# Two Fourier layers in one kernel: the projection of layer 1 takes sum and difference of its two terms

## What is computed

```python
a = x_ft[:, :, :nm, :nm]                      # 32 x 32 modes of the image
blk1 = _complex_matmul_2d(a, fw1)             # [B, O, 32, 32]
blk2 = _complex_matmul_2d(a, fw2)
out_ft = out_ft.at[:, :, :nm, :nm].set(blk1)
out_ft = out_ft.at[:, :, N - nm:, :nm].set(blk2)
out = jnp.fft.irfft2(out_ft, s=(N, M)) / scale_bwd
res = out @ W + b
return jax.nn.relu(res + out)
```

## Time and profile before

| | us |
|---|---|
| median of 3 runs (lowest, highest) | 2138.09 (2133.49, 2140.34) |
| time of the profiled execution | 2134.44 |
| its span in the profile | 2132.6 |
| the part from load 2's issue (763) to the last load's first mix (1018) | 255 |
| from there to the end of the last projections (1046) | 28 |

### The profile page before, as it was taken

How to read it: one execution, slowest core, us unless ns; L and a number is a source line. 1 busy time by engine, 2 the same in 40 slices (tenths; PEclk the granted TensorE clock), 3 DMA queues, 4 the chain that set the end, 5 groups by cost and what they waited for, 6 DMA issues and landing times.

```text
span 2132.6 us, 57900 instructions
## 1 busy us (share of the span) xinstructions
PE 1878.7 (88%) x24558; PEld 1494.5 (70%) x24558; DVE 1426.5 (67%) x2151; ACT 1144.2 (54%) x1869; POOL 282.8 (13%) x526
## 2 busy tenths in 40 slices
PE   5898998999639678888559999999999999999999
PEld 3676766777524567777447888878878788887887
DVE  5876776677144742222267888878888788887887
ACT  5755665556114311111146776666767666776665
POOL 0000000000000210000131304032040501404000
PEclk9999999999855579989879999999999999999999
DMA  8887887786296589999338888888788888888886
GB/s 305 312 262 237 277 266 227 251 271 204 62 155 80 117 238 265 257 264 273 90 127 289 293 301 325 305 321 297 277 310 307 321 307 282 299 305 307 315 308 244
DMA packets 210172, 546.88 MB, mean 256 GB/s; under 512 B 64322, under 2 KB 139586, under 8 KB 173634
## 3 DMA queue, kind: packets, MB, share of 16 engines
q1 hardware_dynamic: 150866, 458.18, 64.0%
q10 hardware_dynamic: 53680, 41.95, 8.0%
q0 software_dynamic: 5376, 43.07, 6.9%
HBM read 361.68 MB, written 148.96 MB: 239 GB/s over the span
## 4 chain that ended last, share of the span: by engine, by line
PE 41%; DMA 8%; DVE 1%; POOL 0%; issue 0%; DVEq 0%; POOLq 0%
PE ps_y L1406 13%; PE ps_xt L1353 9%; PE ps_wave L1392 9%; DMA x_in<-in_x 7%; PE ps_col L1373 5%; PE ps_y L1396 4%; DVE by_channel L770 1%; DVE low_tile L1296 0%; DMA tile<-high_tile 0%; DMA planes_in<-planes 0%; POOL tile L1223 0%; POOL planes_in L1211 0%; DVE by_channel L771 0%; DVE y_out L1325 0%; POOL low_tile L1223 0%
## 5 line engine op out<-in xcount | busy, mean ns | idle before, releaser
L1255 ACT ACTIVATE x_turned<-ps_xt 128x512 f16<-128x512 f32 x512 | 305.6, 597 | 320.4 <-PE ps_xt L1353 320.4
L1406 PE MATMUL ps_y<-apply,x_turned 128*128 128x128 f16 x6144 | 427.9, 219 | 0.0
L1406 PEld LDWEIGHTS ps_y<-apply,x_turned 128*128 128x128 f16 x6144 | 377.2, 98 | 64.5 <-issue 0.5
L1304 DVE TENSOR_TENSOR x_turned<-ps_xt,x_turned 128x512 f16<-128x512 f32 x512 | 351.6, 687 | 94.4 <-ACT x_turned L1255 94.4
L221 DVE TENSOR_TENSOR parts<-stage,parts 128x1024 f16<-128x1024 f32 x256 | 302.0, 1220 | 121.4 <-ACT parts L145 120.9
L1325 DVE SCALAR_TENSOR_TENSOR y_out<-ps_y,relu 128x512 f32<-128x512 f32 x512 | 351.5, 687 | 21.5 <-PE ps_y L1406 1.9
L1353 PE MATMUL ps_xt<-c_eye,x_in 128*128 128x128 f32 x2048 | 311.4, 275 | 10.6 <-DMA x_in<-in_x 10.6
L1265 ACT ACTIVATE relu<-ps_wave 128x512 f32<-128x512 f32 x512 | 303.4, 593 | 14.4 <-PE ps_wave L1392 14.4
L145 ACT ACTIVATE parts<-stage 128x1024 f16<-128x1024 f32 x256 | 255.1, 1049 | 78.8 <-issue 42.5
L290 PE MATMUL row_ps<-parts,c_rows_dft 128*64 128x512 f16 x1536 | 201.8, 391 | 62.8 <-DVE parts L221 53.1
L1296 DVE SCALAR_TENSOR_TENSOR low_tile<-ps_col,high_tile 128x512 f16<-128x512 f32 x248 | 171.1, 691 | 92.2 <-ACT high_tile L1248 92.2
(11 more groups left out here) (129 smaller groups left out, 1888.4 us busy)
## 6 DMA issues: line engine op xcount, KB each, us to landing
stage<-in_x SPq DMA_DIRECT2D x256, 512.0 KB, 4.9
x_in<-in_x SPq DMA_DIRECT2D x128, 1024.0 KB, 10.9
out_y<-y_out SPq DMA_DIRECT2D x128, 1024.0 KB, 7.0
fw_first<-in_fw SPq DMA_DIRECT2D x9, 2048.0 KB, 16.3
fw<-in_fw ACTq DMA_DIRECT2D x8, 2048.0 KB, 19.4
fw<-in_fw SPq DMA_DIRECT2D x8, 2048.0 KB, 17.5
fw_first<-in_fw ACTq DMA_DIRECT2D x7, 2048.0 KB, 20.4
tile<-high_tile POOLq DMA_DIRECT2D x48, 240.0 KB, 13.6
```

Source lines behind the costliest of these rows:

```text
L1255: nc.scalar.activation(turned[u % 2][:, 0, :, :], ps_turn[u % 2][:, :, :], ACT.Copy).then_inc(turn_high, 1)
L1304: nc.vector.tensor_tensor(v[:, 1, :, :], ps_turn[u % 2][:, :, :], v[:, 0, :, :], ALU.subtract).then_inc(turn_split, 1)
L1406: mm = nc.tensor.matmul(ps_y[u % 2][:, :, 2 * k:2 * k + 2], turned[u % 2][:, p, k, :], apply[:, bass.ds(b, 1), q, :, :].rearrange("p o c w ...
```

## The change

The first term and the second term of a frequency k go into the cosine row as their sum and into the sine row as their difference. Before, one matmul for each term made both rows, with 256 columns in `table`. Now DVE makes the sum and the difference (`add`, two instructions on 128x512 f32, into two new buffers `mix_sums`), and a matmul makes one row (h = 0 from the sum, h = 1 from the difference) with 128 columns. The number of matmuls per frequency stays 8; frequency 0 has no second term and reads `mix_turned` as before, frequency 32 has no first term and gets a copy and a negated copy. `table` is half as large. Then the order within a step changes on each engine:

```diff
+            def add(k):
+                if k == 0:
+                    return
+                n = sums_number(k)
+                for f in terms(k):
+                    dve.wait_ge(turn_taken, 2 * (slot_of(f, k) + 1))
+                if n >= 2:
+                    dve.wait_ge(out_ready, number[[j for j in order if j != 0][n - 2]] + 1)
...
+                    nc.vector.tensor_tensor(to[:, 0, :], first, second, ALU.add)
+                    nc.vector.tensor_tensor(to[:, 1, :], first, second, ALU.subtract).then_inc(sums_ready, 1)
@@ sync
             for step in range(STEPS + 8):
+                if step % KC == KC - 1 and step // KC + SL < LOADS:
+                    load(sp, 0, step // KC + SL)
                 for blk in flush_at(step):
                     store(sp, blk, 0, stored)
-                if step % KC == KC - 1 and step // KC + SL < LOADS:
-                    load(sp, 0, step // KC + SL)
@@ scalar
             for step in range(STEPS + 8):
-                for k in project_at(step):
-                    take_high(k)
-                for blk in flush_at(step):
-                    store(act, blk, 1, stored_sin)
                 slot = turn_at(step)
                 if slot is not None:
                     take_turn(slot)
                 if step % KC == KC - 1 and step // KC + SL < LOADS:
                     load(act, 1, step // KC + SL)
+                for k in project_at(step):
+                    take_high(k)
+                for blk in flush_at(step):
+                    store(act, blk, 1, stored_sin)
@@ vector
             for step in range(STEPS + 8):
+                if step < STEPS:
+                    take_mixed(step)
                 for k in project_at(step):
                     take_low(k)
-                if step < STEPS:
-                    take_mixed(step)
+                for k in project_at(step + 1):
+                    add(k)
@@ tensor, project(k)
+                if k == 0:
+                    pe.wait_ge(turn_taken, 2 * (slot_of(0, 0) + 1))
+                else:
+                    pe.wait_ge(sums_ready, sums_number(k) + 1)
...
                 for bh in range(2):
...
+                    for h in range(2):
+                        for r in range(2):
+                            v = turned(slot_of(0, 0))[:, 0] if k == 0 else sums[sums_number(k) % 2][:, h]
+                            last = nc.tensor.matmul(
+                                ps_out[n % 2][:, bh, :, h, :], v[:, r, bh * HB:(bh + 1) * HB, :].rearrange("p b y -> p (b y)"),
+                                table[:, r, h, :, :], start=(r == 0),
+                                stop=(r == 1 and (k, h) != (0, 0)))
@@ tensor
             for step in range(STEPS + 8):
-                for k in project_at(step):
-                    project(k)
                 slot = turn_at(step)
                 if slot is not None:
                     turn(slot)
                 if step < STEPS:
                     mix(step)
+                for k in project_at(step):
+                    project(k)
```

More of the change, by code:

```diff
@@ L837, in mix_project @@
         out = [m.sb(f"project_out{i}", [P, 2, 2, 2, 2, FLUSH, C], F16) for i in range(2)]
-        table = m.sb("project_table", [P, 2, 2, 2, 2, C])
+        sums = [m.sb(f"mix_sums{i}", [P, 2, 2, B, K1]) for i in range(2)]
+        table = m.sb("project_table", [P, 2, 2, 2, C])
         W_eye = m.sb("W_eye", [P, C])
@@ L861, in mix_project, with sums_number @@
         block = m.stack.enter_context(nc.Block())
+        def sums_number(k):
+            return number[k] - (number[0] < number[k])
         def turned(slot):
@@ L932, in take_turn @@
                         before = slot - KC if slot % KC else slot - 2 * KC
+                        if before == 0:
+                            act.wait_ge(out_ready, number[0] + 1)
                         if before >= 0:
-                            act.wait_ge(out_ready, max(number[k] for k in range(K1 + 1) for f in terms(k)
-                                                       if slot_of(f, k) == before) + 1)
+                            act.wait_ge(sums_ready, max(sums_number(k) for k in range(1, K1 + 1) for f in terms(k)
+                                                        if slot_of(f, k) == before) + 1)
                     y0 = i * MG // 2
@@ L1000, in _ @@
                 nc.vector.tensor_tensor(W_eye[half, :], w["W"][half, :], w["eye"][half, half], ALU.add).then_inc(table_cleared, 1)
-            nc.vector.memset(table[:, :, :, :, :, :], 0.0).then_inc(table_cleared, 1)
+            nc.vector.memset(table[:, :, :, :, :], 0.0).then_inc(table_cleared, 1)
             nc.vector.memset(first_y[:, :], 0.0).then_inc(table_cleared, 1)
             dve.wait_ge(table_cleared, 4)
[L1004 to L1011, removed]
+            for r in range(2):
+                for part in range(2):
+                    for h in range(2):
+                        half, g = slice(part * C, (part + 1) * C), (r + part + h) % 2
+                        minus = (r, part) == (1, 1) if h == 0 else (r, part) == (0, 0)
+                        nc.vector.tensor_scalar(table[half, r, h, g, :], W_eye[half, :], -1.0 if minus else 1.0, None,
+                                                ALU.mult).then_inc(table_ready, 1)
             nc.vector.memset(first_y[:, 0::K1], 1.0).then_inc(table_ready, 1)
@@ L1063, in project @@
                 for bh in range(2):
[L1064 to L1069, removed]
-                            stop=((f, r) == pairs[-1] and k > 0))
-                    if k == 0:
-                        last = nc.tensor.matmul(ps_out[n % 2][:, bh, 0, 0, :], first_y[0:1, :], bias_n[0:1, :],
-                                                start=False, stop=True)
+                    for h in range(2):
+                        for r in range(2):
+                            v = turned(slot_of(0, 0))[:, 0] if k == 0 else sums[sums_number(k) % 2][:, h]
[3 more added lines that the diff above has]
+                                stop=(r == 1 and (k, h) != (0, 0)))
+                        if (k, h) == (0, 0):
+                            last = nc.tensor.matmul(ps_out[n % 2][:, bh, 0, 0, :], first_y[0:1, :], bias_n[0:1, :],
+                                                    start=False, stop=True)
                 last.then_inc(out_ready, 1)
             for step in range(STEPS + 8):
-                for k in project_at(step):
-                    project(k)
                 slot = turn_at(step)
```

12 lines of the change are left out of this document (9 added, 3 removed).

## The result

| | before | after |
|---|---|---|
| median of 6 runs each, us (lowest, highest) | 2136.45 (2132.76, 2144.38) | 2154.95 (2149.24, 2166.13) |
| ratio after to before, 95% interval | | 1.0086 (1.0054 to 1.0117) |
| the profiled execution, us; its span | 2134.44; 2132.6 | 2154.77; 2152.8 |
| load 1's issue to the issue of the last stores, from SP's queue | 298.2 | 321.5 |

The changed kernel is slower, as forecast: the forecast was +12.9 us, the medians say +18.5. Inside the block the traces differ by 23.3 us; the stages before it were 3.4 us shorter in that execution (load 1's issue at 743.86 instead of 747.30), so all of the loss is in the block.

What follows compares the result with a forecast made beforehand. Bound: the loop of group, release and transfer through two weight buffers, paced by even groups. Terms 11.9 - 5.0 + 3.2 + 5.6 - 2.0 - 0.8 = +12.9 us gave 2147.3 (median 2151), range 2128 to 2172.

Steps and rivals of the forecast that it cites:

- Projection, pair, chain: PE's projection takes 1.94 us, DVE's pair 1.30, the serial chain from one projection's hand-over to the next's start 2.77.
- Even group: On PE, an even load's group now holds three projections and two chains: 13.8 us against 12.1, +11.9 over seven.
- Clock and stalls: Four more even groups start at 1.2 GHz on PE, +5.6 us; some unexplained stalls fall into idle time, -2.0.
- The two even groups that did not wait for weights: PE arrives 4.6 us earlier per chunk, worth 2.5 at each of these two groups: -5.0.
- Stores ahead of the load: Stores issue about 0.25 us behind the release instead of 0.8 ahead; the load behind is 1.05 later, three times: +3.2.
- End: From the last load's first mix to the issue of the last stores: 26.4 us instead of 27.2, -0.8.
- PE's own work sets the pace: Rival: PE's path over a chunk falls from 30.1 to 27.2 us, so faster, 2120 to 2127; chance 0.23.
- Swallowed: Rival: stalls lie in the new gaps, clock stays up, stores cost nothing; no change, 2138 to 2144; chance 0.18.
- The clock falls inside the groups: Rival: one more projection in each even group runs at 1.2 GHz, 13.6 us on top, 2165; chance 0.17.

Runs made afterwards that it cites:

- e5: The changed kernel with PE's waits ahead of even groups 6, 8, 10, 12 and 14 filled with matmuls that nobody reads; 2151.64 us, 1.0081 of before.
- e1: The changed kernel with DVE making the next frequency's sum and difference ahead of this one's eviction; 2135.81 us, 0.9989 of before.
- e2: The changed kernel with two more DVE instructions ahead of each pair, written to a buffer nobody reads; 2182.48 us, 1.0197 of before.
- e3: The kernel before with only the new order within a step, no sums; 2167.82 us, 1.013 of before.
- e4: The changed kernel (sums and differences) with the old order within a step; 2131.07 us, 0.9968 of before.
- e8: e4 with the pair for the next frequency ahead of this one's eviction on DVE; 2127.35 us, 0.9962 of before.
- e10: e8 with all stores of the 64 steps on SP's queue, a step later, behind the load; 2125.98 us, 0.993 of before.
- e11: The changed kernel with all stores of the 64 steps on SP's queue, behind the load; 2140.66 us, 1.0004 of before.
- e9: e4 with the stores issued one step later on both SP's and ACT's queues, behind the load; 2152.67 us, 1.0081 of before.
- e12: The kernel before, without sums, with all stores of the 64 steps on SP's queue, behind the load; 2136.65 us, 0.9997 of before.
- e6: The changed kernel with the stores issued one step later on both SP's and ACT's queues, behind the load; 2151.33 us, 1.0065 of before.

## Why the prediction was right in sign and 5.6 us short

**Projection, pair, chain: right.** 1.98 for a projection (1.94 forecast). The pair takes 1.28 (1.30); 686 and 684 ns each. The Trainium skill, VectorE: DVE Perf Modes, section on the TRN2 errata, gives 691 ns for such an add, and the trace agrees within about 1%; but the two start 0.59 apart, so that a pair is not twice the row's duration. The chain, from 870.47 to 873.16, is 2.69 (2.77 forecast).

**Even group: right.** 13.8 us at full clock, as e5's three groups show; e1, e2, e3 and e4 each moved the time through this term, in the forecast direction, though e1's even groups got shorter by less than expected, as stalls and the low clock filled part of the room. Seven groups of 13.8 are 96.6 against 84.7 for seven of 12.1: +11.9, as forecast.

**Clock and stalls: right in kind, too small.** This is the term that was most off. What the even groups take above those values grew from 8.3 (93.0 less 84.7) to 16.0 (112.6 less 96.6), +7.7. The forecast had +5.6 for the clock and -2.0 for stalls that hide in new idle time, +3.6. The stalls did not hide: 9.6 us in 9 places before, 9.6 in 3 after, and inside even groups 4.0 and 4.1. So the growth is the clock's, and e5 puts 7.6 us of five groups on it. In before two groups started low (6 and 10, 1.4 us each), in the changed kernel five (6 to 14, by 2.2, 1.3, 1.6, 2.0 and 2.4): three more and not four, but each dearer. The waits that came were longer than the 4.5 on which the term stood (12.37 and 6.87 above), and the first projection, put at 0.75 us, lost 1.6 in group 6 (3.60 above).

**The two even groups that did not wait for weights: this step failed for one of them.** The forecast was -5.0, 2.5 each. In the trace of before they are groups 2 and 12. Group 2 came 2.1 us earlier (*start*, 38.9 to 36.8), nearly as forecast. Group 12 did not: the gap ahead of it went from 20.6 to 21.3, and the three gaps without a store from 20.5, 19.4 and 20.6 to 19.4, 20.1 and 21.3, +0.3 together. Groups 4 and 12 had started only 1.2 us later than a landing of 19.3, so that 2.5 was not to be had at group 12, and the landings of loads 8 and 12 then took 20.1 and 21.2 from issue. A load that PE stood waiting for did not come sooner because PE was early. Why these landings got longer is open. That the odd load now follows 11.4 us behind (876.48 to 887.85) and not 13.2 does not settle it: in e2 load 12, with the next one 11.9 behind, was used after 19.3, and in e1 load 8, with the next one 13.4 behind, after 22.1.

**Stores ahead of the load: right in size, partly by luck.** The forecast was +3.2, and the three gaps with a store went from 78.9 to 81.8, +2.9. But it is made up otherwise. The term took from one row that a store is issued 0.8 us ahead of the release; the other two stood 1.4 and 2.5 ahead, and all three now stand 0.2 behind. So the loads were issued 6.0 us later behind their release (1.7, 1.7 and 2.7), not 3.2, and 3.1 of that came back as shorter landings.

**End: wrong in sign.** It was put at -0.8 and came out at +2.5. PE at the end of the block:

```profile
1049.27 2.05 PE L1097 MATMUL project_ps<-project_table,mix_sums 128*128 128x128 f32 x16
1053.94 3.78 PE L1097 MATMUL project_ps<-project_table,mix_sums 128*128 128x128 f32 x16 [2.61 <-DVE mix_sums L999]
1060.33 5.35 PE L1097 MATMUL project_ps<-project_table,mix_sums 128*128 128x128 f32 x32 [2.61 <-DVE mix_sums L999]
```

Two chains of 2.6 us with nothing beside them were counted; that the projections behind them run at 1.2 GHz (3.78) was not. e1 shows the worth of the chain here: the end took 21.5.

**Rivals.** *PE's own work sets the pace* asked for an even group no longer than before. It did not come about, and its price of 2120 to 2127 wanted more than the chain's removal: e1 gave 2135.81; only with the old order too (e8, e10) does the kernel come to 2127.35 and 2125.98. *Swallowed*: nothing was, see the stalls. *The clock falls inside the groups*: not in groups 6 to 14 of the changed kernel, where only the first projection is slow; in groups 2 and 4 a later one is (3.78 and 3.26), behind stalls of 2.9 and 1.2 us. e2 shows that the clock does fall with waits of 2.1 instead of 1.4.

The sum by what was measured: 11.9 + 7.7 + 3.3 - 2.1 + 2.5 = 23.3 in the block of one execution, of which the forecast had 12.9; the stages before it took 3.4 less in that execution, and the medians differ by 18.5.

## What to carry to other kernels

Where a loop runs from a buffer's release through a transfer to its next use, count only what stands between the first and the last reader of that buffer; work that is halved but moved in there is a loss, and a busy share of 83% on the engine does not tell (e3: +30 us for a move that adds no work). When an operand is made by another engine, put its making ahead of that engine's wait for the previous result (e1: -19 us for two swapped lines). Move stores behind an urgent load only onto a queue whose engine computes nothing (e11: -14 us; e9, the same move on ACT too: +22 us against e4), and see which load then stands behind them (e12 against before, and e10 against e8: nothing gained that is clear of the noise).

## What was not expected of the hardware

- Issuing is not a fixed cost. Four stores of 256 KB took 3.1 to 4.5 us to issue ahead of a 2 MB load (before and after); behind one just issued they took 9.3 to 10.9 on SP and 12.75 to 15.1 on ACT (e6 and e9), and eight on SP 15.4 (e11) to 16.7 (e10). The engine that issues stands still for that time. The reason, full queues or something else, was not measured.
- Two f32 operations back to back on DVE start 0.59 to 0.61 apart (871.21 to 873.02 above) though each shows 0.68 to 0.69.
- The granted clock was 0.52 right behind a wait of 12.37 us and 0.68 on average in a group of e2 with waits of 2.1 inside; with waits of 1.4 inside (865.9 to 876.2 in the changed kernel) it was 1.00:

```profile
865.90:876.20 10.30, 7.51 (x224) 7.00 (x228) 5.31 (x9) 1.79 (x3) 0.00 (x0) 1.00 0.44 77
```
